# Decoder block with routed experts: indirect transfers held between value products, routing choice moved to the start of a step

## What is computed

```python
x = x + attn(layernorm(x), Wq, Wk, Wv, Wo)        # 16 heads of 8, rope, elu+1, causal linear attention
x = x + xattn(layernorm(x), ctx, ctx, mask)       # softmax attention on a context of 64 tokens
x = x + ffn(layernorm(x), ...)                    # shared expert + 2 of 8 routed experts per token

# in ffn
probs = softmax(xn @ gate_w.T)
tk_probs, tk_idx = top_k(probs, 2)
out = swiglu(xf, sWg, sWu, sWd)
for e in range(8):
    out = out + w[:, e:e + 1] * swiglu(xf, Wg[e], Wu[e], Wd[e])
```

## Time and profile before

| | us |
|---|---|
| median of three runs (883.4 to 885.89) | 883.92 |
| the profiled execution: span from first to last instruction | 999.2 |
| first load to step 4 | 0 to about 130 |
| steps 4 to 15 (with transfers of c_scatter) | about 130 to 573 |
| steps 16 to 20, shared expert | about 573 to 727 |
| routed experts | 727 to 977 |
| last loads, sums and stores | 977 to 999.2 |

### The profile page before, as it was taken

The page is one execution under the profiler, slowest core; times in us unless marked ns, Lnnn a source line. Parts: engine busy times, 40 slices in busy tenths (PEclk is TensorE's granted clock), DMA queues, the critical chain, the costliest instruction groups (busy, mean ns, idle before and its releaser), DMA issues.

```text
span 999.2 us, 37214 instructions
## 1 busy us (share of the span) xinstructions
PE 830.2 (83%) x14611; PEld 626.2 (63%) x14611; DVE 661.5 (66%) x1800; ACT 581.6 (58%) x1185; POOL 550.5 (55%) x729
## 2 busy tenths in 40 slices
PE   3788997898898888898787677796989999999991
PEld 2456675666665665566564454685867877777780
DVE  1247786977766976887696396479455555556773
ACT  3568885786675785787685364352345555555450
POOL 5365456757656766666665454238125555555552
PEclk9799999998787998899898696799999999999995
DMA  9211110220210210210221101302212222225665
GB/s 243 50 46 45 46 46 24 62 51 24 62 50 24 62 51 25 63 54 28 57 54 50 32 13 57 104 17 57 54 33 75 77 74 76 78 71 168 195 186 162
DMA packets 96040, 68.56 MB, mean 69 GB/s; under 512 B 9680, under 2 KB 88027, under 8 KB 95872
## 3 DMA queue, kind: packets, MB, share of 16 engines
q1 hardware_dynamic: 84592, 47.95, 18.3%
q0 software_dynamic: 8640, 16.93, 4.8%
q10 hardware_dynamic: 2640, 1.31, 0.4%
HBM read 43.05 MB, written 24.02 MB: 67 GB/s over the span
## 4 chain that ended last, share of the span: by engine, by line
PE 64%; DVE 16%; issue 11%; ACT 6%; DMA 1%; POOL 1%; SPq 0%; another core or an unknown queue 0%; POOLq 0%; ACTq 0%; DVEq 0%
PE bank L875 8%; PE pair_x L857 7%; PE pair_x L573 6%; PE pair_x L664 5%; PE bank L681 5%; PE bank L610 4%; PE bank L490 3%; PE pair_y L857 3%; PE pair_x L740 2%; PE bank L843 2%; PE pair_y L740 2%; PE pair_y L573 2%; DVE Ex L1436 2%; PE bank L752 2%; PE pair_y L566 2%
## 5 line engine op out<-in xcount | busy, mean ns | idle before, releaser
L1333 POOL DMA_INDIRECT mixed<-f_y,f_x x142 | 138.8, 977 | 139.2 <-ACT f_y L1143 82.5
L1241 POOL DMA_INDIRECT routed<-c_row,c_idx x128 | 131.6, 1028 | 41.7 <-issue 41.7
L1202 POOL TENSOR_TENSOR Kblk<-ctxT,con 128x512 f32<-128x512 f32 x64 | 66.9, 1045 | 87.2 <-PE pair_y L573 45.8
L960 ACT ACTIVATE Am<-pair_x 128x1024 f32<-128x1024 f32 x64 | 65.3, 1020 | 73.0 <-PE pair_x L573 73.0
L610 PE MATMUL bank<-Vblk,Am 128*32 128x18 f32 x4096 | 68.9, 190 | 38.7 <-issue 35.4
L573 PE MATMUL pair_y<-Kblk,KQ 32*64 32x256 f32 x1024 | 100.0, 449 | 0.3 <-issue 0.2
L573 PE MATMUL pair_x<-Qblk,KQ 32*64 32x256 f32 x1024 | 97.1, 443 | 2.1 <-issue 2.0
L875 PEld LDWEIGHTS bank<-Qblk,Am 128*128 128x128 f32 x568 | 80.7, 191 | 24.7 <-issue 17.4
L610 PEld LDWEIGHTS bank<-Vblk,Am 128*32 128x32 f32 x4096 | 54.4, 112 | 62.1 <-issue 58.8
L875 PE MATMUL bank<-Qblk,Am 128*128 x568 | 91.7, 284 | 1.2 <-ACT f_y L1143 0.8
L995 ACT COPY ExT<-pair_x 128x1024 f32<-128x1024 f32 x64 | 64.5, 1008 | 48.0 <-PE pair_x L664 47.6
(11 more groups left out here) (210 smaller groups left out, 2142.4 us busy)
## 6 DMA issues: line engine op xcount, KB each, us to landing
f_x<-routed SPq DMA_DIRECT2D x142, 65.0 KB
ctxD<-in_ctx SPq DMA_DIRECT2D x32, 256.0 KB, 4.3
ctxP<-in_ctx SPq DMA_DIRECT2D x16, 256.0 KB, 2.8
maskB<-in_mask_BxS_if SPq DMA_DIRECT2D x16, 256.0 KB, 4.7
Cblk<-mixed SPq DMA_DIRECT2D x16, 256.0 KB
Kblk<-mixed SPq DMA_DIRECT2D x16, 256.0 KB
block_out<-X SPq DMA_DIRECT2D x11, 256.0 KB
mixed<-f_y,f_x POOLq DMA_INDIRECT x142
```

The costliest lines, as they stand in the source:

```text
L1202: return pool.tensor_tensor(dst[:, j, :, :, :], both.to_broadcast([P, 2, RH, T]), rows, ALU.mult)
L1241: pool.indirect_dma_start(routed[:, :], bass.IndirectOffsetOnAxis(ap=c_idx[:, par, t, n:n + 1], axis=0), c_row[:, par, t, n, :], None, bou ...
L1333: pool.indirect_dma_start(mixed[:, :], bass.IndirectOffsetOnAxis(ap=f_x[:, u, D + 1:D + 2].bitcast(I32), axis=0), f_y[:, u, :], None, boun ...
```

## The change

On POOL, `c_scatter` issues one transfer k of the group's eight instead of the two of a tile, and the eight are placed anew: transfers 0 to 2 once the value product 1 of a is done (`values_done`), transfer 3 once product 2 is, transfer 4 once product 3 is, and transfers 5 to 7 in the next step once its first scores are issued (`scores_issued`). The rsqrt for b moves ahead of b's block 2, behind the first three transfers. In the last step and where a is off, the holds for values don't wait; the order stands. On TensorE, `c_positions` moves from behind a's product 1 to the place behind the output projection, ahead of scores 2. On VectorE, `c_second` and `c_weights` move to the start of the step, behind a_divide of h and ahead of the context evacuation, and `c_index` takes the place where c_second was. No instruction that computes or transfers is added or removed.

```diff
--- before.py
+++ after.py
@@ -784,13 +784,13 @@
                     c_positions(d, h)
                 if on(h):
                     a_out(h, f)
+                if not s_is_last(s) and on(d):
+                    c_positions(d, h)
                 shared(s, 2)
                 scores(a, b, 2, par)
                 shared(s, 3)
                 if on(a):
                     a_values(a, 1, par)
-                if not s_is_last(s) and on(d):
-                    c_positions(d, h)
                 if on(f):
                     a_k_T(f, h, d)
                 shared(s, 4)
@@ -1228,19 +1228,19 @@
                                        .to_broadcast([P, GT * 2 * H, HALF]),
                                        ALU.mult).then_inc(S["a_r2"], 1)
 
-            def c_scatter(d, par, t):
-
-                if t == 0:
+            def c_scatter(d, par, k):
+
+                if k == 0:
                     pool.wait_ge(S["c_idxd"], d + 1)
                     pool.wait_ge(S["c_cp"], d + 1)
                     pool.wait_ge(S["c_ch"], C_STEPS * d + C_STEPS)
                     if since(d, 1):
                         pool.wait_ge(S["c_tick"], d)
                     carry_wait(1).then_inc(S["c_tick"], 1)
-                for n in range(TOP):
-                    pool.indirect_dma_start(routed[:, :], bass.IndirectOffsetOnAxis(ap=c_idx[:, par, t, n:n + 1], axis=0),
-                                            c_row[:, par, t, n, :], None, bounds_check=ROWS - 1, oob_is_err=False)\
-                        .then_inc(c_sc[par], 16)
+                t, n = divmod(k, TOP)
+                pool.indirect_dma_start(routed[:, :], bass.IndirectOffsetOnAxis(ap=c_idx[:, par, t, n:n + 1], axis=0),
+                                        c_row[:, par, t, n, :], None, bounds_check=ROWS - 1, oob_is_err=False)\
+                    .then_inc(c_sc[par], 16)
 
             def split_shared_weights():
 
@@ -1260,11 +1260,21 @@
                 pool.wait_ge(S["w_hi"], e + 2)
                 pool.tensor_tensor(wup_lo[:, e, :, :], wup[:, e], wup_hi[:, e, :, :], ALU.subtract).then_inc(S["w_lo"], 1)
 
+            def scores_issued(a, b, j):
+
+                if on(a):
+                    pool.wait_ge(S["a_s"], NP * a + j + 1)
+                elif on(b):
+                    pool.wait_ge(S["b_s"], NP * b + j + 1)
+
+            def values_done(a, j):
+
+                if on(a):
+                    pool.wait_ge(S["a_av"], NP * a + j + 1)
+
             def step(s, par):
                 e, f, a, h, b, c, d = s + 2, s + 1, s, s - 1, s - 2, s - 3, s - BEHIND
                 odd = 1 - par
-                if on(d - 1) and (not s_is_last(s - 1)):
-                    c_scatter(d - 1, odd, 2)
                 if on(e) and (not s_before(s, -1)):
                     rsqrt(e, a_mv, a_rs, a_nm, S['a_ag'], S['a_pw'], S['a_rsd'], S['a_xnd'])
                 if on(a):
@@ -1273,12 +1283,14 @@
                     for n in range(0, 3):
                         split_weights(n)
                 if on(d - 1) and (not s_is_last(s - 1)):
-                    c_scatter(d - 1, odd, 3)
+                    scores_issued(a, b, 0)
+                    for k in range(5, GT * TOP):
+                        c_scatter(d - 1, odd, k)
                 if on(b):
                     b_block(b, 3, par)
                 if s_is_last(s):
-                    for t in range(GT):
-                        c_scatter(d, par, t)
+                    for k in range(GT * TOP):
+                        c_scatter(d, par, k)
                 if on(h):
                     b_block(h, 0, odd)
                 if on(f):
@@ -1289,23 +1301,28 @@
                     rsqrt(c, c_mv, c_rs, c_nm, S['c_ag'], S['c_pw'], S['c_rsd'], S['c_xf'])
                 if on(a):
                     a_block(a, 3, par)
+                if not s_is_last(s) and on(d):
+                    values_done(a, 1)
+                    for k in range(3):
+                        c_scatter(d, par, k)
                 if on(h):
+                    rsqrt(h, b_mv, b_rs, b_nm, S['b_ag'], S['b_pw'], S['b_rsd'], S['b_xnd'])
                     b_block(h, 2, odd)
                 if on(c):
                     c_variance(c)
                 if s_is_last(s):
                     for n in range(3, 6):
                         split_weights(n)
-                if on(h):
-                    rsqrt(h, b_mv, b_rs, b_nm, S['b_ag'], S['b_pw'], S['b_rsd'], S['b_xnd'])
                 if not s_is_last(s) and on(d):
-                    c_scatter(d, par, 0)
+                    values_done(a, 2)
+                    c_scatter(d, par, 3)
                 if isinstance(s, int) and s == GROUPS:
                     split_shared_weights()
                 if on(f):
                     a_block(f, 1, odd)
                 if not s_is_last(s) and on(d):
-                    c_scatter(d, par, 1)
+                    values_done(a, 3)
+                    c_scatter(d, par, 4)
                 if s_is_last(s):
                     for n in range(6, 8):
                         split_weights(n)
@@ -1624,6 +1641,9 @@
                     c_second(d)
                 if on(h):
                     a_divide(h, 1)
+                if not s_is_last(s) and on(d):
+                    c_second(d)
+                    c_weights(d, par)
                 if shared_of(s, 1) + 1 in range(GROUPS):
                     s_low(shared_of(s, 1) + 1)
                 if on(h):
@@ -1647,7 +1667,7 @@
                 if shared_of(s, 2) in range(GROUPS):
                     s_hidden(shared_of(s, 2))
                 if not s_is_last(s) and on(d):
-                    c_second(d)
+                    c_index(d, par)
                 if on(f):
                     a_rotate(f)
                 if s_is_last(s) and on(d):
@@ -1663,8 +1683,6 @@
                     s_hidden(shared_of(s, 3))
                 if shared_of(s, 3) + 1 in range(GROUPS):
                     s_low(shared_of(s, 3) + 1)
-                if not s_is_last(s) and on(d):
-                    c_index(d, par)
                 if s_is_last(s):
                     tiles(0)
                 if on(b):
@@ -1682,8 +1700,6 @@
                     s_low(shared_of(s, 5) + 1)
                 if shared_of(s, 4) in range(1, GROUPS + 1):
                     s_add(shared_of(s, 4) - 1)
-                if not s_is_last(s) and on(d):
-                    c_weights(d, par)
                 if shared_of(s, 5) in range(GROUPS):
                     s_hidden(shared_of(s, 5))
                 if on(a):
```

## The result

The change made the kernel slower: 902.19 us (median of 4 runs, 901.43 to 904.7) against 883.66 us for the kernel before beside it, a ratio of 1.0208 with a 95% interval of 1.0164 to 1.0252. The profiled execution took 901.62 us with a span of 899.8, so 1.8 us lie around the span.

A forecast was written before the change was run, and what follows sets the result against it. In the profile, TensorE's small matmuls were taken to stand still while POOL issues indirect transfers, mostly absent from timed runs. The forecast was 883.92 - 12.7 - 1.1 + 21.0 = 891.1 us, range 850 to 910.

The forecast's parts named there:

- How much of it exists in a timed run?: Of the profile's TensorE stalls beside POOL's transfers, a share of 0.15 was taken to exist in timed runs.
- part 1: POOL's transfers held between value products: 84.5 and 7.2 us saved in the profile, 12.7 and 1.1 us timed.
- The holds: POOL's waits keeping transfers off TensorE's products: 12.7 us saved over twelve steps, 1.1 us in the late steps, timed.
- In an undisturbed step they don't fit: Without VectorE's pause, the moved chains delay the context evacuation, so scores 1 wait 1.75 to 2.2 us.
- part 3: Routing choice and weights early on VectorE: cost between 0 and 3.5 us a step, 1.75 taken, 21.0 us in all.
- The sum: Timed median 883.92 us less 12.7 and 1.1 for held transfers, plus 21.0 for early chains: 891.1 us.
- Covered by 1.5 us, cost 0: Behind POOL's hold for the first scores, c's statistics are ready by 142.3 and ScalarE uses them at 143.84: cost 0.
- part 2: Waits added on POOL, for the first scores and for products 1 to 3: cost 0.
- The span of about 928 us: Profile span after the change: 999.2 less 84.5 and 7.2 for stalls, plus 21.0 for VectorE's moved chains.
- Rival 1: TensorE's stalls hold in timed runs, so faster: 813 us at full share, 859 us at half; chance 0.34.
- Rival 3: POOL late to the first scores' hold, ScalarE's norm of c waits: 12 us more, 903 us; chance 0.14 with Rival 4.
- Rival 4: Held transfers fall onto the products of b, so the profile keeps broken products; chance 0.14 together with Rival 3.

The follow-up runs named there:

- chains_early_3: The change's early routing choice and weights, with POOL's program as in the kernel before, on kind A: 941.6 us, 1.0682 of the kernel before.
- second_ahead_2: The same kernel as second_ahead, run again on kind A: 880.53 us, 0.9994 of the kernel before.
- windows: The change with c_second, c_weights behind b's shifts, two transfers behind next scores 0, two behind scores 1, none behind product 3; kind B: 954.37 us, 0.9523.
- after_again: The whole change, unmodified, run again beside the kernel before on kind B: 949.42 us, ratio 0.9451.
- second_ahead: The kernel of windows with c_second alone put back ahead of the context evacuation, on kind B: 937.6 us, 0.93 of the kernel before.

## Why the prediction was right, and where it was wrong

The forecast was 891 us, slower by 0.8%, at a chance of 0.47 for slower; measured are 902.19, slower by 2.1%, inside the range. Its mark, slower in time with a much shorter span, came true, but the shorter span had another reason than the one given, and that the time fell into the range owes something to luck.

**"How much of it exists in a timed run?" (part 1).** This step failed. It took the span of 999.2 and the median of 883.92 for two executions of one thing and put the missing 115.3 us on the capture. Every execution whose time and span are both on record has its time 1.8 to 1.9 us above its span, on both kinds of chip. The stalls are real on kind B and nearly absent on kind A, in executions that were profiled all the same. Beside transfers, a value product of a lasts 3.39 us in the mean in the profile of before, and 1.05 us in chains_early_3, which has the same transfers in the same places on kind A. So a share of 0.15 of the stalls, on the chip that was timed, is close to what there is (0.26 of 2.60 us above 0.79, a share of 0.10), for a wrong reason: that is luck. The rule of the Trainium skill ("Runtime: NRT & Kernel Launch", The ~15us preamble/postamble breakdown), that a profile's total exceeds the reported time by some 6 us whatever the kernel, was set against this. The runs agree that the gap is small and constant; in size and sign they differ, since here the time is the longer one, by 1.8 to 1.9 us over the span. What the Trainium skill ("NOTIFIC — the notification-queue block", 7.1) says of the block that writes the records explains nothing here.

**The holds (part 1).** Sized at 12.7 + 1.1 us. On kind A the change is 39.4 us faster than the chains alone. Little of that is products: it is the pause before L490 and the clock behind it. Against the kernel before no saving shows there: second_ahead_2, with the transfers held and the chains' wait nearly gone, takes 0.9994 of its time (0.9952 to 1.0036), so 4 us at most net where 13.8 were counted. It has waits of its own, though (9.3 us in ten for the rotation from 134 to 560 us), which may hide a part. What the holds alone do on kind A wasn't measured, nor was the kernel before profiled there.

**"In an undisturbed step they don't fit" (part 3).** Right in mechanism, and in size beside the change's own order of transfers. The evacuation follows the chain without idling, and TensorE waits for it: in the steps with a projection at L490, which runs ahead of scores 1 and which the step had not named, 15.3 us in ten waits, 1.4 us a step of the eleven where 1.75 was taken; from 487 us on, where no projection is left, at scores 1 for b's subtraction, as it was put, 9.7 us in 5 waits. In second_ahead_2, which has c_weights late and the transfers in the places of windows, these are 2.0 and 3.3 us. With 1.4 us for the one projection at half clock that is 15.3 + 9.7 - 2.0 - 3.3 + 1.4 = 21.1 us, and the times differ by 902.19 - 880.53 = 21.7 (the profiled spans by 24.7), where 12 x 1.75 = 21.0 were forecast. The two kernels ran on different occasions and differ in more than c_weights, so the agreement is not a proof. The step forecast at about 31.5 us measured 31.80, and 30.11 in second_ahead_2.

What the term didn't say is that it depends on POOL's order: beside the old one the same chains cost 59.8 us.

**The sum.** +21.0 and -13.8 give +7.2, against +18.5 measured. If the chains cost the 21 us that the waits add up to, the term that was mis-sized is the holds' saving, some 3 us instead of 13.8. But the two terms are no independent parts: taken one after the other they are +59.8 for the chains and -39.4 for the holds added to them.

**"Covered by 1.5 us, cost 0" (part 2).** Right as far as the rows go. In one step of the change the values from c's statistics are ready at 206.88 and ScalarE uses them at 209.42 without idling. TensorE's weight loads wait for a block of POOL twice from 134 to 560 us, 6.9 us, both at the end (487 and 543 us) and both together with a wait for b's subtraction that is counted above.

**The span of about 928 us.** Measured 899.8. It was a forecast for a chip of kind B, where the change's span was 950.0: there 84.5 + 7.2 - 21.0 = 70.7 us were to be saved and 52.9 were (1002.29 - 949.42).

**Rival 1** (the stalls hold, faster, 813 to 859 us) is what happens on kind B, at 52.9 us of its 71. **Rival 3** (slower through POOL) shows in no row of the change. **Rival 4** did in part, on kind B: beside transfers the change's products of b still last 1.91 us in the mean against 0.82 without, one of them the product behind the single transfer (229.14 to 231.11 in after_again). Windows moves that transfer away.

## What to carry to other kernels

Before a saving is split into "in the profile" and "in the run", compare a stage that the change can't touch, and the granted clock, between the profile and the runs: when they disagree by 10%, suspect two chips or sessions before the profiler, and ask for a profile and a time of one execution. Work that is moved ahead of an evacuation is cheap as long as the engine has slack there: here 1.3 us of it left waits of 2.0 us in eleven steps, 3.0 to 4.0 us left 15.3, and 5 us left 40.1, with TensorE's clock lost on top. A new order of POOL's transfers has to be judged together with VectorE's order, because each sets where the other's gaps are.

## What the runs showed that I had not expected

- The same program takes 881 us on two chips and 1002 to 1021 us on four. The granted clock of the kernel before is 0.95 to 0.97 on the former and 0.89 to 0.92 on the latter. On the latter, small matmuls (128x18) stop again and again while POOL issues indirect transfers: a value product of a (64 matmuls) beside transfers takes 3.4 to 3.6 us in the mean instead of 0.8, with transfers of the same length (0.98 us) and pitch. Whether it is the issuing or the moving of the data that stops them no run separates. What tells the chips apart wasn't found, and whether a chip keeps its kind wasn't tried; the kernel before was profiled on kind B alone.
- So one change can be 2.1% slower on one chip and 5.5% faster on another. The version in second_ahead shows no loss against the kernel before on either (0.9994 and 0.93), and by its ratios better than the change on both (1.0208 and 0.9451), each taken on another chip.
- The clock was at 1.2 GHz behind pauses of 2.8 to 4.5 us in a TensorE stream that was otherwise full, each time for 3.4 or 6.8 us, and so over the projection behind the pause: 38.5 us of such pauses cost some 16.7 us more in the projections alone. Of two pauses of 2.4 us one had this effect.
- VectorE's operations of 0.2 us with both inputs in its own memory last until POOL's block of 1.04 us beside them ends (48 of 48), those that read a bank don't (nine of nine).
